# Tables and scaled weights of the second stage, made while the state-space layer opens

## The reference

```
x = _layernorm(x + mamba(x))                     # state-space layer
x = _layernorm(x + depool(x, ctx, lens, ...))    # early stage, first part
x = _layernorm(x + ternary(x, weight, g, b))     # early stage, second part

depool:  bidx = cumsum(patch_lens) - 1                       # ends of patches
         boundary_mask[b, bidx] = 1
         plug = clip(cumsum(boundary_mask) - 1, 0, 127)
         s_t = a * s_(t-1) + u_t,  u from rmsnorm(ctx) * g_init
         out = s[plug] + (rmsnorm(x) * g_res) @ W_in.T + b_in
ternary: w_q = round(clip(w / mean|w|)) in {-1, 0, 1}
```

## Time and profile before

| | |
|---|---|
| time, median of 3 runs | 3107.66 us (3099.18 to 3108.26) |
| time of the profiled execution | 3109.04 us |
| its span | 3107.3 us |
| PE busy, share of the span | 2736.4 us, 88% |
| DVE busy | 1633.2 us, 53% |
| ACT busy | 1438.5 us, 46% |
| POOL busy | 1411.4 us, 45% |
| state-space layer | 0 to 563.2 us |
| early stage | 563.5 to 694 us |

### The profile page before, as it was taken

How to read it: one execution, slowest core, us unless ns; L and a number is a source line. 1 busy time by engine, 2 the same in 40 slices (tenths; PEclk the granted TensorE clock), 3 DMA queues, 4 the chain that set the end, 5 groups by cost and what they waited for, 6 DMA issues and landing times.

```text
span 3107.3 us, 70976 instructions
## 1 busy us (share of the span) xinstructions
PE 2736.4 (88%) x25057; PEld 2133.0 (69%) x25057; DVE 1633.2 (53%) x3568; ACT 1438.5 (46%) x4586; POOL 1411.4 (45%) x1644
## 2 busy tenths in 40 slices
PE   6888888559989978979995889999996996999999
PEld 6777776436756656755664767877874675768888
DVE  4998899564446655561115763333333223555643
ACT  4666655344456656743335862223221334772310
POOL 3777777442356765543335661323332223663320
PEclk8999999779999999979997989999996998999999
DMA  2000000210000000041112020000007111011100
GB/s 82 3 3 2 3 3 2 63 36 1 23 12 17 14 23 1 22 168 44 46 41 76 0 93 8 11 10 7 10 19 250 33 31 53 1 48 29 52 9 20
DMA packets 75147, 106.19 MB, mean 34 GB/s; under 512 B 11024, under 2 KB 54672, under 8 KB 74656
## 3 DMA queue, kind: packets, MB, share of 16 engines
q1 hardware_dynamic: 68960, 86.68, 8.5%
q0 software_dynamic: 5952, 16.26, 1.7%
HBM read 88.50 MB, written 14.42 MB: 33 GB/s over the span
## 4 chain that ended last, share of the span: by engine, by line
PE 55%; POOL 5%; DVE 4%; issue 3%; ACT 3%; DMA 1%; SPq 1%; DVEq 0%; ACTq 0%; POOLq 0%
PE up_ps L2439 5%; PE e_out_ps L2457 5%; PE t_ps L634 4%; PE s_ps L620 3%; PE bank_a L1508 3%; PE bank_b L1508 3%; POOL probs L539 2%; PE up_ps L2433 2%; PE bank_a L582 2%; PE bank_d L671 2%; ACT probs L758 2%; PE frame_ps L1587 2%; PE bank_d L590 2%; PE bank_b L1524 2%; PE bank_a L1524 2%
## 5 line engine op out<-in xcount | busy, mean ns | idle before, releaser
L539 POOL TENSOR_TENSOR probs<-probs,inv 128x512 f32<-128x512 f32 x320 | 328.3, 1041 | 282.0 <-DVE inv L863 281.8
L3351 POOL TENSOR_TENSOR hc<-h,bc 128x1024 f32<-128x1024 f32 x128 | 302.2, 2361 | 120.0 <-DVE h L3623 91.9
L758 ACT ACTIVATE probs<-s_ps,negmax 128x128 f32<-128x128 f32 (+1 forms) x768 | 297.7, 415 | 7.8 <-DVE negmax L823 6.3
L3623 DVE TENSOR_TENSOR_SCAN h<-da,dbu_ps 128x1024 f32<-128x1024 f32 x128 | 292.5, 2285 | 11.4 <-DVE dbu_ps L3635 4.4
L634 PE MATMUL t_ps<-ident,probs 128*128 128x128 f32 x1280 | 209.2, 287 | 58.8 <-POOL probs L539 50.4
L634 PEld LDWEIGHTS t_ps<-ident,probs 128*128 128x128 f32 x1280 | 140.0, 142 | 125.8 <-POOL probs L539 60.5
L3440 PE MATMUL dta_ps<-dt,a_spread 32*128 32x128 f32 x2048 | 160.0, 297 | 66.9 <-ACT da L3570 39.2
L3570 ACT ACTIVATE da<-dta_ps 128x1016 f32<-128x1016 f32 x128 | 130.3, 1018 | 152.1 <-PE dta_ps L3440 151.8
L3440 PEld LDWEIGHTS dta_ps<-dt,a_spread 32*128 32x128 f32 x2048 | 134.7, 199 | 89.4 <-ACT da L3570 39.5
L2366 POOL DMA_INDIRECT expert_rows_out<-y,row_to x62 | 61.2, 987 | 268.6 <-DVE y L2718 138.2
L823 DVE TENSOR_REDUCE negmax<-s_ps 128x4 f32<-128x1024 f32 (+1 forms) x128 | 156.6, 1223 | 44.9 <-PE s_ps L620 43.2
(11 more groups left out here) (511 smaller groups left out, 6772.3 us busy)
## 6 DMA issues: line engine op xcount, KB each, us to landing
cT<-in_ctx_turned SPq DMA_DIRECT2D x32, 256.0 KB, 2.7
w_down<-in_L_ffn_w SPq DMA_DIRECT2D x8, 1024.0 KB, 11.8
w_up<-in_L_ffn_w SPq DMA_DIRECT2D x8, 1024.0 KB, 13.0
c_in<-in_ctx SPq DMA_DIRECT2D x16, 256.0 KB, 2.8
w_gate<-in_L_ffn_w SPq DMA_DIRECT2D x8, 512.0 KB, 6.5
w_up<-in_L_ffn_w SPq DMA_DIRECT2D x8, 512.0 KB, 9.0
w_down<-in_L_ffn_w SPq DMA_DIRECT2D x8, 512.0 KB, 8.9
w_gate<-expert_rows_out SPq DMA_DIRECT2D x8, 512.0 KB, 7.8
```

What stands on the lines that cost most here:

```text
L539: pool.tensor_tensor(probs[:, u % 2, i], probs[:, u % 2, i], inv[:, u % 2, HB * i:HB * (i + 1)].unsqueeze(2).broadcast_to([P, HB, W]), ALU ...
L758: last = act.activation(probs[:, u % 2, i, k, :], src, ACT.Exp, bias=negmax[:, u % 2, at], accum_out=sums[:, u % 2, at])
L3351: pool.tensor_tensor(hc[:, s % 4], h[:, s % 2], bc[:, j, 1, :].unsqueeze(1).broadcast_to([P, 2 * G, P]), ALU.mult).then_inc(hc_ready.sem, 1)
L3623: dve.tensor_tensor_scan(flat(h[:, s % 2]), flat(da[:, s % 4]), dbu_ps[s % 2][:, :, :, :].rearrange("p i g t -> p (i g t)"), 0.0, ALU.mult ...
```

## The change

All tables, scaled weights and rounded weights of the early stage move into a class `EarlyTables`. Its pieces are put between the instructions of the state-space layer's opening, before the scan. They borrow what the opening does not use yet: the four banks of `dbu_ps` and one of `dta_ps`, and the state buffers `hc` (one-hot and `plugged` tables) and `h` (the turned ones). What must last (`spread`, the scaled weights, `w_q`, the bias rows) has memory of its own on the other side. DVE instead of ACT copies `spread` out of the banks. In place the weights `w_in` are scaled where they lie. The early stage then starts with its loop and its four context loads.

```diff
+class EarlyTables:
...
+    def lend(self, banks, spare_bank, hot, plugged, turned):
+        flat = lambda bank: bank.rearrange("p g t -> p (g t)")
+        self.banks, self.tiny, self.spare = banks, flat(banks[0]), flat(spare_bank)
+        self.hot, self.plugged, self.plugged_T = hot, plugged, turned
+    def load_ends(self, sp):
+        for dst, src in self.by_ends:
+            sp.dma_start(dst, src).then_inc(self.ends_loads.sem, 16)
+    def load_others(self, sp):
+        for dst, src in self.others:
+            sp.dma_start(dst, src).then_inc(self.loads.sem, 16)
+    def sum_lens(self, pe):
+        pe.wait_ge(self.ends_loads.sem, self.ends_in)
+        pe.wait_ge(self.step.sem, self.step.done(0))
+        pe.matmul(self.tiny[:, 0:B], self.upto[:, :], self.lens[:, :], start=True, stop=True
+                  ).then_inc(self.product.sem, 1)
+    def sum_hits(self, pe):
+        pe.wait_ge(self.core.setup.sem, self.core.setup.base)
+        pe.wait_ge(self.hot_made.sem, self.hot_made.done(0))
+        for b in range(B):
+            last = pe.matmul(self.tiny[:, B + b:B + b + 1], self.hot[:, b, :], self.core.ones[:, 0:1], start=True, stop=True)
+        last.then_inc(self.product.sem, 1)
+    def make_spread(self, pe):
+        pe.wait_ge(self.plugs_made.sem, self.plugs_made.done(0))
+        for g, bank in enumerate(self.banks):
+            for k in range(4):
+                last = pe.transpose(bank[:, k, :], self.plugged[:, 4 * g + k, :], self.core.ident[:, :])
+            last.then_inc(self.turned.sem, 1)
+        pe.wait_ge(self.w_step.sem, self.w_step.done(1))
+        pe.matmul(self.spare[:, 0:1], self.core.ones[:, :], self.w_sum[:, :], start=True, stop=True
+                  ).then_inc(self.product.sem, 1)
+        for g, bank in enumerate(self.banks):
+            pe.wait_ge(self.copied.sem, self.copied.done(g))
+            pe.matmul(bank.rearrange("p g t -> p (g t)"), self.decay[:, :],
+                      self.plugged_T[:, 4 * g:4 * g + 4, :].rearrange("p b t -> p (b t)"), start=True, stop=True
+                      ).then_inc(self.spread_made.sem, 1)
+    def find_ends(self, dve):
+        dve.wait_ge(self.ends_loads.sem, self.ends_in)
+        dve.tensor_copy(self.lens[:, :], self.lens_i[:, :]).then_inc(self.step.sem, 1)
+        dve.wait_ge(self.product.sem, self.product.done(0))
+        dve.tensor_scalar(self.last_at[:, :], self.tiny[:, 0:B], -1.0, None, ALU.add).then_inc(self.step.sem, 1)
+        dve.wait_ge(self.step.sem, self.step.done(1))
+        dve.tensor_scalar(self.wrapped[:, :], self.last_at[:, :], 0.0, float(P), ALU.is_lt, ALU.mult
+                          ).then_inc(self.step.sem, 1)
+        dve.wait_ge(self.step.sem, self.step.done(2))
+        dve.tensor_tensor(self.ends[:, :], self.last_at[:, :], self.wrapped[:, :], ALU.add).then_inc(self.step.sem, 1)
+        dve.wait_ge(self.step.sem, self.step.done(3))
+        dve.wait_ge(self.numbered.sem, self.numbered.done(0))
+        for b in range(B):
+            last = dve.tensor_scalar(self.hot[:, b, :], self.number[:, :], self.ends[:, b:b + 1], None, ALU.is_equal)
+        last.then_inc(self.hot_made.sem, 1)
+    def plug_in(self, dve):
+        dve.wait_ge(self.product.sem, self.product.done(2))
+        dve.tensor_scalar(self.plug0[:, :], self.tiny[:, 2 * B:3 * B], -1.0, 0.0, ALU.add, ALU.max
+                          ).then_inc(self.step.sem, 1)
+        dve.wait_ge(self.step.sem, self.step.done(5))
+        dve.tensor_scalar(self.plug[:, :], self.plug0[:, :], float(P - 1), None, ALU.min).then_inc(self.step.sem, 1)
+        dve.wait_ge(self.step.sem, self.step.done(6))
+        for b in range(B):
+            last = dve.tensor_scalar(self.plugged[:, b, :], self.number[:, :], self.plug[:, b:b + 1], None, ALU.is_equal)
+        last.then_inc(self.plugs_made.sem, 1)
+        dve.wait_ge(self.loads.sem, self.others_in)
+        dve.scalar_tensor_tensor(out=self.w_abs[:, :, :], in0=self.w[:, :, :], scalar=-1.0, in1=self.w[:, :, :],
+                                 op0=ALU.mult, op1=ALU.max).then_inc(self.w_step.sem, 1)
+        dve.wait_ge(self.w_step.sem, self.w_step.done(0))
+        dve.tensor_reduce(self.w_sum[:, :], self.w_abs[:, :, :], AX.XY, ALU.add).then_inc(self.w_step.sem, 1)
+        _, over_dt, times_dt = depool_constants()
+        dve.tensor_scalar(self.g_init2[:, :], self.g_init[:, :], over_dt, times_dt, ALU.mult, ALU.mult
+                          ).then_inc(self.scaled.sem, 1)
+        for cc in range(DC):
+            dve.tensor_scalar(self.w_in[:, cc, :], self.w_in[:, cc, :], self.g_res[:, cc:cc + 1], None, ALU.mult
+                              ).then_inc(self.scaled.sem, 1)
+    def take_spread(self, dve):
+        for g, bank in enumerate(self.banks):
+            dve.wait_ge(self.turned.sem, self.turned.done(g))
+            dve.tensor_copy(self.plugged_T[:, 4 * g:4 * g + 4, :], bank).then_inc(self.copied.sem, 1)
+        dve.wait_ge(self.product.sem, self.product.done(3))
+        dve.tensor_scalar(self.mean_w[:, :], self.spare[:, 0:1], 1.0 / (D * D), None, ALU.mult).then_inc(self.w_step.sem, 1)
+        dve.wait_ge(self.w_step.sem, self.w_step.done(2))
+        dve.tensor_scalar(self.inv_w[:, :], self.mean_w[:, :], 1e-5, None, ALU.add).then_inc(self.w_step.sem, 1)
+        for g, bank in enumerate(self.banks):
+            dve.wait_ge(self.spread_made.sem, self.spread_made.done(g))
+            dve.tensor_copy(self.spread[:, 4 * g:4 * g + 4, :], bank).then_inc(self.spread_copied.sem, 1)
+    def round_weights(self, dve):
+        rounding = 1.5 * 2.0 ** 23
+        dve.wait_ge(self.w_step.sem, self.w_step.done(3))
+        dve.reciprocal(self.inv_w[:, :], self.inv_w[:, :]).then_inc(self.w_step.sem, 1)
+        dve.wait_ge(self.w_step.sem, self.w_step.done(4))
+        dve.tensor_scalar(self.wq[:, :, :], self.w[:, :, :], self.inv_w[:, :], rounding, ALU.mult, ALU.add
+                          ).then_inc(self.w_step.sem, 1)
+        dve.wait_ge(self.w_step.sem, self.w_step.done(5))
+        dve.tensor_scalar(self.wq[:, :, :], self.wq[:, :, :], -rounding, 1.0, ALU.add, ALU.min).then_inc(self.w_step.sem, 1)
+        dve.wait_ge(self.w_step.sem, self.w_step.done(6))
+        dve.tensor_scalar(self.wq[:, :, :], self.wq[:, :, :], -1.0, None, ALU.max).then_inc(self.w_step.sem, 1)
...
 def depool_ternary_stage(...)
         def sync(sp):
-            for dst, src in by_ends:
-                sp.dma_start(dst, src).then_inc(ends_loads.sem, 16)
-            for b in range(2):
+            for b in range(4):
                 sp.dma_start(c_in[:, b % 4, :], context[b]).then_inc(c_landed[b % 4].sem, 16)
-            for dst, src in by_in:
-                sp.dma_start(dst, src).then_inc(in_loads.sem, 16)
...
 def mamba_stage(...)
         def sync(sp):
+            tables.load_ends(sp)
             sp.dma_start(xT[:, :, 0:2, :], x_turned[:, :, 0:2, :]).then_inc(first_in.sem, 16)
             sp.dma_start(w_in_sb[:, :, :], chunked(w_in)).then_inc(first_in.sem, 16)
             for dst, src in plain:
                 sp.dma_start(dst, src).then_inc(loads.sem, 16)
+            tables.load_others(sp)
...
+            tables.sum_lens(pe)
             pe.wait_ge(first_in.sem, first_in.base + 32)
             project(0, 0, front, u_made)
             project(1, 0, y_ps, u_made)
+            tables.sum_hits(pe)
             project_z(0, front)
...
             project_z(1, y_ps)
+            tables.sum_plugs(pe)
             pe.wait_ge(prep.sem, prep.done(2))
...
             step_sizes(0, 0)
+            tables.make_spread(pe)
+            pe.wait_ge(tables.w_step.sem, tables.w_step.done(2))
             spread_out((0, 0, 0), None)
+            pe.wait_ge(tables.spread_copied.sem, tables.spread_copied.done(3))
             spread_out((0, 0, 1), (0, 0, 0))
...
+            tables.find_ends(dve)
             dve.wait_ge(loads.sem, weights)
...
+            tables.take_hits(dve)
...
+            tables.plug_in(dve)
+            tables.take_spread(dve)
             weigh_inputs((0, 0, 0))
+            tables.round_weights(dve)
             dve.wait_ge(rest_in.sem, rest_in.base + 32)
             every_sequence(dve, unit)
```

238 lines of the change are left out of this document (86 added, 152 removed).

## The result

| | before | after |
|---|---|---|
| time, median | 3105.03 us (3098.06 to 3109.93, 20 runs) | 3098.6 us (3093.16 to 3106.1, 20 runs) |
| ratio | | 0.9984, 95% interval 0.9977 to 0.9991 |
| span of the profiled execution | 3107.3 us | 3104.3 us |
| first weighing, first scan | 43.74, 45.17 | 50.39, 53.05 |
| last `yT` of the layer | 555.1 | 566.5 |

A forecast was written before the change was run, and what follows sets the result against it. Latency of one DVE and PE chain bounds the early stage's start; DVE paces the state-space layer. −19.4 − 0.4 + 4.0 = −15.8 from 3109.04 gave 3093.2, or 3092 on the median's scale; range 3088 to 3096, for all cases 3082 to 3104.

The forecast's parts named there:

- Removed part, −19.4: Head of the early stage: with the table work gone, the first `t` comes 19.4 us sooner, bounds 15.7 to 20.8.
- The third step's −0.4: Early stage's third step: DVE loses reciprocal and rounding, 1.61 us, of which 0.4 was taken as gain.
- Rival 2: Early loop gets slower without the filling work that lifted PE's clock: +2 to +5 us, time up to 3097; chance 0.12.
- SP, +1.34: Layer's opening: three table loads ahead of `xT` and `w_in` delay PE's start by 1.34 us.
- One-column products, +3.4: Layer's opening: 32 PE passes take 3.72 us, 3.4 net on the chain ahead of the third projection.
- rival 1: One-column products count as idleness, so the opening's rest runs at half clock: about −7 us, time 3101; chance 0.13.
- Transposes and decay products, hidden: Layer's opening: about 6.3 us of PE work fits the 7.64 us wait for POOL's `dt`, costing nothing.
- The clock gives back 1.9: First two half steps: PE, busy during the wait for `dt`, keeps its high clock, saving 1.04 and 0.85 us.
- the rule on transposes: Skill rule that transposes don't count as busy for PE's clock; by it 1.9 us wouldn't return, opening +5.9.
- DVE's rounding, +1.2: Between first weighing and first scan: rounding of 1.61 us counted as +1.2, between 0.6 and 1.6.
- Sum of the opening: State-space layer's opening: 1.34 + 3.4 − 1.9 + 1.2 = +4.0 us, bounds 2.5 and 13.4.
- Rival 4: State-space layer's scan settles into more half clock: 25 half steps cost 22 us, time 3114; chance 0.06.

The follow-up runs named there:

- e2: The changed kernel, cut off behind the state-space layer with the 16 sequences stored there: 587.85 us.
- e8: The changed kernel cut behind the early stage, with two unused 512-column products on PE between decay products and first half step: 699.28 us.
- e14: The kernel before, cut behind the state-space layer, plus sixteen unused f32 one-column products and 32 instructions on PE that only wait: 579.52 us.
- e17: The changed kernel, cut behind the state-space layer, with PE's loop over the 12 middle sequences written out: 564.22 us.
- e4: The changed kernel, cut off behind the early stage with the 16 sequences stored there: 696.94 us.
- e5: The changed kernel cut behind the early stage, with the sixteen one-column products made 128 columns wide: 696.92 us.
- e7: The changed kernel cut behind the early stage, with DVE's rounding of weights put before the first weighing of inputs: 699.65 us.
- e9: The kernel before, cut behind the state-space layer, plus sixteen unused f32 one-column products between second and third projection: 599.67 us.
- e16: The kernel before, cut behind the state-space layer, with PE's loop over the 12 middle sequences written out: 556.27 us.
- e1: The kernel before, cut off behind the state-space layer with the 16 sequences stored there: 576.74 us.
- e15: The changed kernel with bf16 one-column products, cut behind the state-space layer, plus 32 instructions on PE that only wait: 581.56 us.
- e11: The full changed kernel with one-hot tables and one-column products in bf16, nothing else: 3088.19 us, ratio 0.9943.
- e12: The full changed kernel with bf16 one-hot products, table loads and sums moved to where engines waited, and rounding before the first weighing: 3094.83 us.
- e18: The full changed kernel with bf16 one-column products and PE's loop in the state-space layer written out: 3076.29 us, ratio 0.9903.
- e13: The kernel before, cut behind the state-space layer, plus 64 instructions on PE that only wait, ahead of its wait for `w_in`: 598.33 us.

## Why the prediction was wrong

Two steps failed. The opening costs 7.9 us instead of 4.0, because the clock fell twice where the forecast had it at full level. And the layer behind the opening, which I had left at its length, takes 3.5 us more in the profiles. A third part is lost behind the early stage. Step by step:

- **Removed part, −19.4.** Right: 19.5. The chain through load, squares, root, `u` and `t` came out within 0.3 us at each step. The third step's −0.4 was measured as 0.4. Rival 2, a slower early loop, fell: 7.77 us a pair.
- **SP, +1.34.** Right: PE starts 1.39 later.
- **One-column products, +3.4.** Their length was right in this profile (3.63 against 3.72). What follows them wasn't: in the changed kernel, and in e2, e8, e14 and e17, the clock is at 0.50 from about 18 to 25 us, and here the convolution costs 2.2 us more. In e2 and e17 the fall comes earlier and takes in the products (4.54 and 4.44) and the third projection (3.76 instead of 2.03) too. In e4, e5, e7 and e9, with the same passes, it stays at 1.00, and in none of the bf16 kernels does it fall there. This is rival 1 in part, present in some executions: what separates them I can't say. By the row of 12 to 18, no idleness of PE came before it. That rival 1's time (3101) lies nearer to the measured one than the forecast's is luck: it had the whole rest of the opening at half clock and 13.1 us for it, while the transposes ran at full clock (16 in 1.96 us).
- **Transposes and decay products, hidden.** Right: POOL's `dt` still comes last, from 44.03 to 45.29. They end 2.1 us ahead of the first half step, not at it.
- **The clock gives back 1.9.** Failed. The first half step takes 1.67 instead of the 1.04 forecast, and from 46 on the clock is at 0.50. PE was busy up to 43.25 and waited 2.14 us ahead of that half step, where the forecast had it without a pause. What came back was 0.38 us (the first weighing is 6.65 later, the first half step 7.03). By its number the rule on transposes, which the prediction had set against this term, came out here, but not by its mechanism: the clock was at 1.00 all through the transposes and the decay products, and with the wait filled (e8) it stayed there. The wait of 2.14 us was the cause, as far as one profile of e8 shows.
- **DVE's rounding, +1.2.** Right: 7.88 − 6.65 = 1.23. Whether moving it gains anything, e7's times can't tell.
- **Sum of the opening.** 1.39 + 5.64 − 0.38 + 1.23 = 7.9, where 5.64 is the shift between PE's start (+1.39) and the first half step (+7.03). By e17 against e16: 8.0. It varies with the clock: the first scan comes at 50.41 in e4, at 53.05 in the changed kernel and at 56.06 in e2, against 44.8 to 46.4 in the four kernels without the change's opening. Forecast 4.0, bounds 2.5 and 13.4 (the working has no terms for the 2.5; the lowest that it names give 3.4).
- **The length of the layer behind the opening, the other step that failed.** I took it as unchanged, so that the opening's shift adds once, since DVE paces it. With PE's loop written out that is true to 1.1 us (490.0 to 491.1). With the loop it isn't: the same scan takes 505 to 528 us, by where 64 or 32 instructions without any work have put the loop's code. The change moved it from 1385 to 1512 instructions and PE's idle at a jump from 1.99 to 2.52; the body grew by 3.5. How much of these 3.5 the place has is argued and not shown. The bodies of e1 and e2 are equal (512.2 and 512.1), and no kernel moves the loop from 1385 to 1512 by waits alone; e15 does so from 1480 (+8.1). Rival 4 had the form of it (more half clock in the layer, decided by PE) and the wrong cause, a phase between sequences.
- **What is left.** −19.5 − 0.4 + 11.4 = −8.5 at the end of the early loop, and the profiles agree (−8.55 at 599.38). The medians of the full kernels differ by 6.4. The two profiled executions differ by 9.1 us up to 1144 us and by 3.0 at the end. 3.3 of it are lost between 1144 and 1165 and some 3 between 2325 and 2400, in stages that are the same in both. At the first place PE's clock differs. Its last four passes in a stage, before and then after:

```profile
1146.21 1.13 PE L671 MATMUL bank_d<-wo,aT 128*128 128x256 f32 x4 [0.40 <-DVE aT L856]
...
1137.80 2.08 PE L671 MATMUL bank_d<-wo,aT 128*128 128x256 f32 x4 [0.40 <-DVE aT L856]
```

In e11, e12 and e18 they take 2.08, 2.08 and 2.07 us. The later loops' jumps don't show as the reason: behind 560 us PE has two waits over 1.2 us ended by "issue" in either profile, 3.03 and 3.97 before, 2.78 and 3.97 after. So here, too, time was lost at the lower level of the clock, in four changed kernels and not in the one before. That is one execution of each, and what lowers it is open.

Two of the prediction's signs caught this: it expected the block's end 3 to 5 us later (it was 11.4), and it named a layer over 8 us longer as what would make it wrong. The trace of before already had the 2 us at 141.49 with "issue" at their end, in a stretch that I had read only by its mean clock of 0.97. The Trainium skill, "Runtime: NRT & Kernel Launch", section "Instruction fetch mechanics", says that a taken branch whose target isn't in the loaded window makes the engine wait for its code, and that code is loaded in blocks of 256 instructions. The traces agree with the first: 1.6 to 3.0 us at each jump, and none at these places with the loop written out. The size of a block no run here shows; e9's second stretch, 12 passes behind the jump, is what such a block's end would look like. Those 12 passes are 26 instructions in the built program, so the stretch begins at the 1475th, and the loops that begin behind that place, at 1480 or 1481, don't have it. That is an argument, not a test.

## What to carry to other kernels

A wait that ends with "issue" once in each turn of an engine's loop, behind its jump, can be the price of that jump, and then it changes with code that is put anywhere ahead of it. The name alone proves nothing (POOL's waits here), and the wait can carry another name (`h` in the changed kernel); that it goes when the loop is written out is the test. Before believing that an edit of the opening slowed or sped up a loop, compare the idle time at the jump, or put in instructions without work and see whether the loop answers; here 64 of them cost 22 us (6 of these ahead of the first scan), more than the whole change was worth. Where a loop is short in count, write it out for the engine that the others wait for: it brought 12 us to the full kernel, twice what moving the tables did.

## What the runs showed that was not expected

- The jump costs more than its idle time: 5 × 1.92 us of idle made 20.5 us of time (e1 against e16). Between 60 and 470 us the mean clock is 0.96 with the loop and 1.00 without, and DVE's waits for products of PE fall from 30.8 us (15.7 of them for `dbu_ps`) to 12.7.
- 128 satisfied waits of PE, 64 instructions, took 6.7 us (start at 13.51 instead of 6.85), 0.1 us each. The 32 by which e13 has more than e14 (10.08) took 3.4.
- A pass with f32 weights costs nearly the same with 1 column (3.63 us for 32) as with 128 (3.74), and 16 passes in bf16 take 0.54.
- The clock can fall right behind work that keeps PE busy (changed kernel, 12 to 25 us), in some executions and not in others of the same code ahead of it (e2 and e4).
